# Loading block sums before the last runs are out, counting by quarters, and unread TensorE products in layers 2 to 4 of a four-layer graph network

## What is computed

```
h = relu(layernorm(x))
layer 1: x += clip(h + segment_sum(h[src]*w*weight, dst) + h*slw, 0, 1)
layer 2: msg = sum over 16 hats b_u*b_v*(h[dst] @ W[u,v]);  x += segment_sum(msg, src)
layer 3: msg = relu(ln(h))[..] with W = edge_attr @ We + be, both directions; plus h @ Wr + bias
layer 4: m = silu(einsum(h[dst], edge_attr_8, W_msg_tp)) @ W_msg_lin
         agg = segment_sum(m, src); u = silu(einsum(h, agg, W_upd_tp)) @ W_upd_lin; x += u
```

## Time and profile before

| | before |
|---|---|
| median of 3 runs | 5112.3 us (5087.6 to 5128.2) |
| profiled execution | 5145.5 us, its span 5143.8 us |
| busy share of the span | PE 44%, LDWEIGHTS 31%, DVE 54%, ACT 23%, POOL 53% |
| POOL gathers (L487) | 1760, mean 947 ns |
| POOL scatters (L469) | 782, mean about 1006 ns |
| unread products (L545) | 1080 MATMUL, 331.9 us |
| granted TensorE clock | 0.688 of full speed on average |

### The profile page before, as it was taken

The page is one execution under the profiler, slowest core; times in us unless marked ns, Lnnn a source line. Parts: engine busy times, 40 slices in busy tenths (PEclk is TensorE's granted clock), DMA queues, the critical chain, the costliest instruction groups (busy, mean ns, idle before and its releaser), DMA issues.

```text
span 5143.8 us, 30784 instructions
## 1 busy us (share of the span) xinstructions
PE 2267.1 (44%) x8710; PEld 1601.6 (31%) x8710; DVE 2773.4 (54%) x4101; ACT 1188.9 (23%) x2921; POOL 2750.7 (53%) x2767
## 2 busy tenths in 40 slices
PE   1110036767622100344444226666641455444998
PEld 0000025555511000233333114444431344333444
DVE  8200944545500006355555856767675566565998
ACT  0000012222201102233333323333332223222011
POOL 4777345555577771555555044555523555543787
PEclk6555567878755555677777657777775777777999
DMA  5000112222310012122223412222242222223010
GB/s 148 9 8 8 28 61 84 94 76 94 84 22 22 13 24 84 51 87 80 79 80 81 124 51 77 85 84 85 84 114 79 82 82 82 82 82 92 22 36 29
DMA packets 192782, 345.70 MB, mean 67 GB/s; under 512 B 81018, under 2 KB 159466, under 8 KB 164067
## 3 DMA queue, kind: packets, MB, share of 16 engines
q1 hardware_dynamic: 106128, 290.26, 15.4%
q0 software_dynamic: 81344, 21.38, 5.9%
q10 hardware_dynamic: 5140, 32.09, 1.6%
HBM read 66.26 MB, written 277.24 MB: 67 GB/s over the span
## 4 chain that ended last, share of the span: by engine, by line
another core or an unknown queue 28%; DVE 25%; PE 19%; issue 18%; ACT 3%; POOL 3%; SPq 2%; DMA 1%; DVEq 0%; POOLq 0%
DVE natS L1197 7%; PE psK L570 6%; PE psX L719 4%; PE psK L566 4%; DVE work L1177 3%; PE psX L545 2%; ACT work L829 1%; POOL natD L511 1%; DVE natD L1197 1%; DVE work L1197 1%; DVE h L1087 1%; SPq L430 1%; DVE psX L1084 1%; PE psX L643 1%
## 5 line engine op out<-in xcount | busy, mean ns | idle before, releaser
L487 POOL DMA_INDIRECT rows<-table,rec x1760 | 1666.9, 947 | 1932.5 <-DMA table<-h 508.7
L1197 DVE SCALAR_TENSOR_TENSOR natS<-natS,keep,psK 128x256 f32<-128x256 f32 x1320 | 634.4, 481 | 639.6 <-remote 468.9
L570 PE MATMUL psK<-work 128*128 128x256 f32 x2640 | 787.0, 451 | 425.5 <-issue 196.9
L570 PEld LDWEIGHTS psK<-work 128*128 128x128 f32 x2640 | 595.0, 233 | 576.4 <-issue 385.9
L829 ACT ACTIVATE work<-iota,rec 128x128 f32<-128x128 f32 x1760 | 536.3, 391 | 793.3 <-remote 611.3
L1177 DVE TENSOR_TENSOR work<-at_hi,psX 128x2048 f32<-128x2048 f32 x220 | 502.4, 2284 | 4.2 <-issue 0.4
L469 POOL DMA_INDIRECT edges_by_dst<-natD,pos x391 | 393.3, 1006 | 181.3 <-issue 126.9
L469 POOL DMA_INDIRECT edges_by_src<-natS,pos x391 | 393.1, 1005 | 130.2 <-issue 130.2
L545 PE MATMUL psX<-keep,ident 128*128 128x256 f32 x1080 | 331.9, 431 | 254.3 <-issue 251.0
L566 PE MATMUL psK<-work 128*128 128x128 f32 x1760 | 300.1, 350 | 136.4 <-DVE work L1177 111.0
L719 PE MATMUL psX<-natD,work 128*128 128x512 f32 x784 | 348.3, 596 | 23.6 <-DMA work<-scan_by_column 15.5
(11 more groups left out here) (158 smaller groups left out, 2590.6 us busy)
## 6 DMA issues: line engine op xcount, KB each, us to landing
scan<-natS SPq DMA_DIRECT2D x110, 1024.0 KB
scan_by_column<-natS SPq DMA_DIRECT2D x55, 1024.0 KB
scan<-natD SPq DMA_DIRECT2D x28, 1024.0 KB
rows<-table,rec POOLq DMA_INDIRECT x1760
scan<-work SPq DMA_DIRECT2D x27, 1024.0 KB
table<-h ACTq DMA_DIRECT2D x28, 896.0 KB, 3.6
work<-scan SPq DMA_DIRECT2D x147, 128.0 KB, 2.1
rec<-edges_by_dst SPq DMA_DIRECT2D x110, 84.0 KB
```

What stands on the lines that cost most here:

```text
L487: pool.indirect_dma_start(out=rows[k][:, u * D:(u + 1) * D], out_offset=None, in_=table.ap(), in_offset=bass.IndirectOffsetOnAxis(ap=rec[k ...
L570: k = nc.tensor.matmul(psK[:, o:o + BW], lo, spread[par][:, o:o + BW], start=True, stop=True)
L1197: V.scalar_tensor_tensor(acc[par][:, t * BW:(t + 1) * BW], was, keep[s][:, q * G + t:q * G + t + 1], psK[:, t * BW:(t + 1) * BW], ALU.mult ...
```

## The change

Four things. (1) SP loads the block sums of chunk 0 as soon as PE's sums are done (`summed`) and all but the last run are out; the last run's store follows chunk 0's loads, and each chunk waits only for the groups that its blocks can lie in. So that nothing is overwritten, layer 4's first accumulator moves to `work[7168:9216]`, layer 3's `sq2` likewise, and ACT waits for the last runs before the update. (2) `sort` builds `OH` in four quarters, each with its own signal, and PE's first 56 products wait for a quarter at a time. (3) `keys(1)` moves behind the four quarters of `sort(0)`; the addition that makes the next slice's base moves behind the slice's own signal. (4) Unread products: `spin(2)` and `spin(3)` behind the halves of `sums` in layers 2 and 4, `spin(4)` behind `lower_sums` in layer 3.

```diff
-                    for g in range(GROUPS - RING - 1, GROUPS):
-                        keep_run(g)
-                    for g in (GROUPS - 2, GROUPS - 1):
-                        sp.wait_ge(run_out[g % 2], kept_runs(l, g))
+                    def runs_out(g):
+                        for q in (g - 1, g):
+                            sp.wait_ge(run_out[q % 2], kept_runs(l, q))
...
+                    for g in range(GROUPS - RING - 1, GROUPS - 1):
+                        keep_run(g)
+                    sp.wait_ge(e["summed"], GROUPS * G)
+                    for c in range(NCH):
+                        if c == 1:
+                            keep_run(GROUPS - 1)
+                        runs_out(max(GROUPS - 2, (T - 1 - (NB - PER * (c + 1))) // G))
+                        block_sums(c)
...
-                pe.wait_ge(in_block, s + 1)
...
+                        if w is allones:
+                            pe.wait_ge(in_block, 4 * s + (b + 1))
...
                             lower_sums(g)
+                            spin(4)
...
-                            if l == 0:
-                                spin(4 + 2 * half)
+                            spin(2 + half if l else 4 + 2 * half)
...
-                for j in range(NBS):
-                    own.did(V.tensor_scalar(OH[:, j, :], keyb[s], float(j), None, ALU.is_equal))
-                own.settle()
-                V.tensor_tensor(OH[:, :, ET:EC], ...).then_inc(in_block, 1)
+                for b in range(4):
+                    own_rows = slice(b * JB, (b + 1) * JB)
+                    for j in range(b * JB, (b + 1) * JB):
+                        own.did(V.tensor_scalar(OH[:, j, :], keyb[s], float(j), None, ALU.is_equal))
+                    own.settle()
+                    V.tensor_tensor(OH[:, own_rows, ET:EC], ...).then_inc(in_block, 1)
+                if s == 0:
+                    keys(1)
...
```

More of the change, by code:

```diff
@@ L182, in build_gnn @@
         assert nat_at <= NAT * FD, nat_at
-        sq2 = natS[:, 0:CW]
+        sq2 = work[:, 7168:7168 + CW]
         small2 = natS[:, 4096:4096 + 4 * CH]
@@ L192, in build_gnn @@
         halves = [prod[:, i * 512:(i + 1) * 512] for i in range(4)]
-        accs = [[prod, work[:, 6144:8192]]] + [[natS[:, i * 2048:(i + 1) * 2048] for i in range(2)]] * 3
+        in_natS = [natS[:, i * 2048:(i + 1) * 2048] for i in range(2)]
+        accs = [[prod, work[:, 6144:8192]], in_natS, in_natS, [work[:, 7168:9216], in_natS[1]]]
         psK = ctx.enter_context(nc.psum_tensor("psK", [P, 2048], f32))
@@ L413, in _, with block_sums @@
                             keep_run(g - 1)
-                    for g in range(GROUPS - RING - 1, GROUPS):
-                        keep_run(g)
-                    for g in (GROUPS - 2, GROUPS - 1):
-                        sp.wait_ge(run_out[g % 2], kept_runs(l, g))
-                    for c in range(NCH):
+                    def runs_out(g):
+                        for q in (g - 1, g):
+                            sp.wait_ge(run_out[q % 2], kept_runs(l, q))
+                    def block_sums(c):
                         if l < 3:
@@ L943, in step @@
                     store_out(c - 1)
+            for g in (GROUPS - 2, GROUPS - 1):
+                act.wait_ge(run_out[g % 2], kept_runs(3, g))
             step(0, True)
@@ L1010, in sort @@
             def sort(s):
-                for j in range(NBS):
-                    own.did(V.tensor_scalar(OH[:, j, :], keyb[s], float(j), None, ALU.is_equal))
-                own.settle()
-                V.tensor_tensor(OH[:, :, ET:EC], OH[:, :, ET:EC],
-                                padmask[:, None, :].to_broadcast([P, NBS, 2]), ALU.mult).then_inc(in_block, 1)
+                for b in range(4):
[3 more added lines that the diff above has]
+                    own.settle()
+                    V.tensor_tensor(OH[:, own_rows, ET:EC], OH[:, own_rows, ET:EC],
+                                    padmask[:, None, :].to_broadcast([P, JB, 2]), ALU.mult).then_inc(in_block, 1)
+                if s == 0:
+                    keys(1)
+                    V.sem_inc(unstaged, 1)
+                    V.sem_inc(copied, 1)
                 A, B, C, I = tiny
@@ L1056, in sort @@
                     own.did(V.tensor_tensor(value.rearrange("p (b j g) -> p b j g", b=4, g=GS), hit, now, ALU.mult))
-                    if v < VS - 1:
-                        own.did(V.tensor_tensor(nxt, hit, now, ALU.add))
                     own.settle()
@@ L1067, in sort @@
                                            ALU.mult, ALU.add).then_inc(places[s], 1)
+                    if v < VS - 1:
+                        own.did(V.tensor_tensor(nxt, hit, now, ALU.add))
+                        own.settle()
                 dve.wait_ge(masks, MASKS)
@@ L1298, in _ @@
             keys(0)
-            keys(1)
-            V.sem_inc(unstaged, 1)
-            V.sem_inc(copied, 1)
             sort(0)
```

## The result

The changed kernel took 5057.4 us (median of 5 runs, 5052.2 to 5086.0), the kernel before 5120.0 beside it (5 runs, 5087.6 to 5128.2): ratio 0.9895, 95% interval 0.9859 to 0.9931, so 1.05% faster. The forecast was 5052. The profiled execution spans 5084.2 us against 5143.8, 59.6 us less. Ratios with an interval leave out the executions of a kernel that took over 1.5% more than its fastest, which in the set of e8 to e11 leaves 5 of the 25 of before (one took 5064), so I also give the quotient of the medians of all executions there. The table gives where the 59.6 us went, stretch by stretch, from the two profiled executions. "Last run" is DVE's last addition of a layer's groups; "the end" is the issue of the last store, 4.0 us ahead of the end of the span.

What follows compares the result with a forecast made beforehand. No engine is full outside the last stage; while POOL issues indirect DMAs, the others run slowly and see signals late. Terms -52 - 13.6 + 6 = -60 us gave 5052 against the median of 5112.3, range 4930 to 5160.

Steps and rivals of the forecast that it cites:

- First sort, -12: First sort: quarters let DVE reduce 10.3 us sooner, POOL starts near 45.5 instead of 57.5; the next stage doesn't wait for it.
- Second sort, -52: Second sort: PE starts near 155 instead of 217.25, full count 62 us sooner; 52 us taken after a charge for slices.
- The rival that quarters don't pay: Second sort: DVE's four waits and late signals eat the earlier start; -20 us, 5092; chance 0.14.
- Block sums, -13.6: After layers 1 to 4: chunk 0 starts sooner, gaining 2, 3.5, 3.5 and 4.6 us.
- the node stage is then bound by DVE: Block sums after layer 2: chunk 1 comes one store later, yet 3.5 us of the 4.6 gained are left.
- Unread products, +6: Layers 2 to 4: 45 us lost in layer 2, 39 gained in layer 4, nothing in layer 3.
- the third group falls out of the cycle: Layer 2: late products turn cycles of three groups into two, 15.3 us a group, 45 us lost.
- its four stand behind the sums and beside DVE's 10.4 us a group; I take nothing: Layer 3: the four unread products a group were taken to cost or gain nothing.
- Clock: PE's clock: the unread products are meant to buy it, but nothing was put in the sum; granted clock 0.50 in layer 1's stops.
- a granted clock over 0.6 inside a stop: PE's clock during POOL's stops: listed among the signs that would show the forecast wrong.
- The rival of paced gathers: Gathers: POOL pauses about 2 us after every group and no backlog builds; -186 us at best, 4926; chance 0.20.
- The slower rival: Layers 2 to 4: signals behind the unread products come a group later in all three; +74 us, 5186; chance 0.18.

Runs made afterwards that it cites:

- e8: Changed kernel, but POOL holds the first placement at its column 64 until PE has counted the second sort: median 5103.8 us, ratio 0.998.
- e11: The changed kernel run again, unchanged: 5113.4 us beside 5158.9 for the kernel before, ratio 1.000.
- e1: Kernel before with only the part on the two sorts (quarters, moved second keys, moved addition): 5083.8 us, ratio 0.9868.
- the second hold: A wait added to the changed kernel: POOL starts the second placement only when layer 1's last group is added up; alone 5074.3 us.
- e4: Changed kernel without the unread products of layers 2 to 4 (layer 1 keeps its own): 5066.0 us, ratio 0.9776.
- e3: Kernel before with only the unread products of layers 2 to 4 added: 5198.5 us, ratio 1.0061.
- e9: Changed kernel, but POOL starts the second placement only when the last group of layer 1 has been added up: 5074.3 us, ratio 0.989.
- e2: Kernel before with only the part on the block sums: 5123.4 us, ratio 0.9942.
- e15: Changed kernel with POOL held in both placements; of the unread products in layers 2 to 4, only layer 2's five a group kept: 5027.4 us, ratio 0.9720.

## Why the prediction was right, and where only its sum was

- **First sort, -12: right, and no term of the sum.** First scatter 45.17 (forecast near 46).
- **Second sort, -52: mechanism right, size too small.** The line of 224 instructions from PE's start gave 443 for the full count, and 437.5 came. The signal came 68.3 us sooner, not 62, since PE began at 149.80 and not near 155. I then charged 8 us for slices beside the placement (62 less 8 is 54; I wrote 52); the first gather came 63.1 us sooner (forecast 51.6), so only 5 us were lost on the way. e1 confirms the gain at 63.6 us, ratio 0.9868. The rival that quarters don't pay is out.
- **Layer 1: a term I did not have.** 13.8 us were lost from gather to gather: 11.4 in the gathers themselves (765.6 us against 754.2, where one cycle had six groups) and 2.4 behind them. The eight kernels without the second hold spread from 1389 to 1426 us, and the spread does not follow the edits: e1 lost nothing, e4 31. Behind the last gather it follows how many groups are left to crawl beside the placement: with 4.1 or 4.5 left the first gather of layer 2 comes 624 to 637 us after the last of layer 1, with 4.9 or 5.0 left 637 to 639, with 5.5 left (e3, e4, e11) 654 to 657. That the link is the cause is argued; that the crawl costs time is shown by e9.
- **Block sums, -13.6: near.** After layers 2, 3 and 4: -2.5, -4.9, -4.6 (forecast 3.5, 3.5, 4.6), in e2 -4.1, -5.0, -4.4. After layer 2 the step "the node stage is then bound by DVE" was wrong: DVE already waited 1.56 us for chunk 1 before, so what the store adds in SP's queue goes straight into the wait (3.32). The 2 us after layer 1 drown in the spread.
- **Unread products, +6: all three sizes were wrong, and the miss is hidden in the one profile.** In layer 2 the step "the third group falls out of the cycle" is right (11 cycles of two, with 16 gathers), but pairs take 28.8 to 30.3 us and the forecast's 30.7 only in e3, and not all cycles become pairs: +18 in the mean of four profiles with against four without (819.2 and 801.5 us), not +45. In layer 4 the shift from two to three groups came, worth 14 us (805.2 in six profiles against 819.3 in eight), not 39. I took 49 groups at 0.8 us from one cycle of 41.3 us (41.1 by its own two ends); the cycles of three take 42.4 us in the changed kernel, some pairs stay, and before had five cycles of three already. In layer 3 the step that failed is "its four stand behind the sums and beside DVE's 10.4 us a group; I take nothing". They stand ahead of the next group's transposes as well, ACT answers these 4 to 10 us later instead of about 1, and the products slide out of the burst into the stop: stops of 10.5 instead of 8.8 us, +47 us in five of six profiles (859.7 against 812.6, the mean of the six without any but e15), and +16 only in the first profile of the changed kernel. The three layers together are +51 us in these means, +43 in e3's profile, and e3 is +37 between medians; the forecast was +6.
- **Clock: half right.** That it would buy nothing was right. That it would stay low in a stop was not, and by my own list a granted clock over 0.6 inside a stop was a sign of being wrong. These windows of a stop of layer 2 (2418.42 to 2430.55) in the changed kernel show it:

```profile
2422.00:2424.00 2.00, 1.89 (x9) 1.89 (x10) 1.51 (x4) 1.97 (x9) 0.00 (x0) 0.50 0.00 0
...
2428.00:2430.00 2.00, 2.00 (x11) 1.75 (x10) 1.89 (x5) 0.00 (x0) 0.00 (x0) 1.00 0.14 27
```

  PE starts at 2422.11, after 17.06 us without a product, at 0.50 as in the earlier trace rows, and is granted 1.00 some 6 us later. But so it is in the kernel before, which has no unread products in layer 2: there PE starts at 2430.06 and has the full clock at 2436.

```profile
2436.00:2438.00 2.00, 1.78 (x11) 1.33 (x9) 1.89 (x5) 0.18 (x1) 0.00 (x0) 1.00 0.12 27
```

  So the sign doesn't speak for the unread products: in this stop they brought the clock back no sooner.

That the time agreed this well is luck. In the profiles the sort brought 11 us more than its term, layer 1 lost 13.8 where 2 were to be gained, and the three layers with unread products came to +1.7 us instead of +6; these misses cancel. And +1.7 is a draw: the same code has +58 in e11. Without the unread products the change would have been better still, by e4's ratio of 0.9776. The rival of paced gathers did not decide, but its pattern is real (layer 3 of e15). The slower rival had layer 3's mechanism, signals that come later behind the unread products, but layer 4 went the other way.

## What to carry to other kernels

While one engine issues many indirect transfers, count the instructions of the others in a handoff, not their duration, and see whether holding that engine for some 30 us lets the others finish: one wait brought the next stage 94 us forward here, of which 39 us were left at the end. An instruction put in to raise a clock stands in a queue; if the kernel stops and goes, look for the signal that ends the stop and for what stands ahead of it in that queue, also well before the stop begins. And where cycles of different length alternate, one profile is a draw from a spread of 20 to 40 us a stage, so a term is read from several kernels that share the stage.

## What was not expected of the hardware

- POOL's scatters stretch the time from PE's first of 112 products to DVE's use of them from 24 us (137.61 to 161.40 in e8) to 288 us, and loads of block sums from 1.06 us (7.42 us for 7, POOL just starting) to 7.5 us each (e9). Whether it is issuing or transfers that does it, and whether taking the profile adds to it, is open.
- The stop and go is not forced. With pauses of about 2.3 us between all groups no stop occurs (e15, 24 groups at 12.2 us); after a pause of 1.29 us the stops return. This was seen once. A kernel that paces POOL on purpose was not tried.
